# Four heads side by side in the value products of the second attention, softmax sums through GpSimd

## The chip, the cores and the metric

The kernel runs on one core of a Trainium2 chip. The metric is the device time of one execution in microseconds (us), lower is better. The median of three runs before the change is 3160.71 us (3154.86 to 3165.05).

## The reference

Eight blocks work on a residual `x` of 4 batches x 1024 tokens x 128 channels. Two of them are attentions with 16 heads. The change is in the second:

```python
def _L1_attn_a_ref(x_bld, Wq, Wkv_down, Wk_up, Wv_up, Wout):   # H, HD = 16, 64; latent 32
    q_blhd = jnp.einsum('bld,dhk->blhk', x_bld, Wq)
    latent_bll = jnp.einsum('bld,dc->blc', x_bld, Wkv_down)
    k_blhd = jnp.einsum('blc,chk->blhk', latent_bll, Wk_up)
    v_blhd = jnp.einsum('blc,chk->blhk', latent_bll, Wv_up)
    attn = jnp.einsum('bqhd,bkhd->bhqk', q_blhd, k_blhd) / jnp.sqrt(HD)
    attn = jax.nn.softmax(jnp.where(causal, attn, neg_inf), axis=-1)
    y_blhd = jnp.einsum('bhqk,bkhd->bqhd', attn, v_blhd)
    return jnp.einsum('bqhd,hdo->bqo', y_blhd, Wout)
```

## The kernel before

The blocks run one after another. Both 16-head attentions are the function `attention` with different settings (`Cfg`). In the second the up-projections are folded into the queries and the output weights, so keys and values of all heads are the same 32 latent channels (`d` = 32).

A **group** is `G` heads of one batch. `probs` holds exp(scores) transposed: a row is a key, a column a query. The keys go in 8 blocks `kb` of 128. Block `kb` has queries from `kb*128` on, so its width falls from 1024 to 128 columns, 4608 columns per head in all. The engines meet in this pattern, in which each engine's order is written out by hand:

- TensorE, per `kb`: for each head the scores (bf16; two products per half that add up pieces of the operands, and a mask product, L833, L835, L838), beside them row-maximum products for later groups (L801, into the two banks of `mx`), then `values(kb-1)` in f32 (L855). There head `j` writes the output partitions `M*j` to `M*(j+1)`, so `128/M` heads stand side by side. After block 4 `turn_max` transposes the maxima of the next group (L812).
- ScalarE: the exp of each head and block into `probs` (L910).
- VectorE: maxima of the next groups (L931 for full tiles, L935 for masked ones), then at block 4 a chain of four small steps (`finish_max`, L945 to L952) on which `turn_max` waits (`s_mc`), copies of the turned maxima (L958), and at a group's end the copy of `outp` to `osb` (L993).
- SyncE: loads up to three groups ahead, and stores.
- GpSimd does nothing inside `attention` but memsets at its start.

The sum of a row of the softmax comes from the value product itself: `vop` has the `d` value columns, one column of ones behind them (L787), and zeros up to `M`. The first attention has `G=4, M=32` with `d=8`. The second has `d=32`, which with the ones column is 33 columns, and so `G=2, M=64`. There are 16 groups of four heads in the first attention, and 32 groups of two in the second. Three batches run in a hardware loop, the fourth is unrolled behind it. In both, every group does all products of its own heads and those of the maxima of as many later heads. Before the first group lies a stretch in which only maxima are computed (24 units for the first group, 8 for the second, with `G=2`; both numbers go with `G`). A unit is one product of up to 512 columns and its maximum.

Of the kernel before, what the change touches and what calls it, by code (L numbers as in the profile page):

```python
# [606 lines left out]
class Cfg:  # L607
# [3 lines left out]
    def __init__(self, G, M, HR, SR, d, scale, k_per_head):  # L611
        self.G, self.M, self.HR, self.SR, self.d, self.scale, self.k_per_head = G, M, HR, SR, d, scale, k_per_head
        self.GN = 16 // G
        self.KG = G if k_per_head else 1
        self.rows = [(96 + 3 * HR if SR else 96), (98 + 3 * HR if SR else 98)]
        self.base = [96, 98] if SR else [0, 0]


def attention(nc, k, tag, cf, qp, kp, qs, ks, vsrc, o_scr, l_scr, m_scr):
# [9 lines left out]
    MU = 12 * G + 2  # L629

# [3 lines left out]
    NARROW_U, WIDE_U = 4 * G, 8 * G  # L634
    NPC = 8 * 4
    with ExitStack() as st:  # L636
# [5 lines left out]
        probs = c.sb("probs", [P, 2, G, T])  # L642
# [5 lines left out]
        osb = c.sb("osb", [P, 2, T])  # L648
        masked = c.sb("masked", [P, 2, CH], BF16)
# [14 lines left out]
        s_dpassed = c.sem("vector_passed")  # L664
        block = st.enter_context(nc.Block())
# [31 lines left out]
        def ahead(b, g, m):  # L697

            if isinstance(b, int) and b == NB - 1 and g + m >= GN:
                return None  # L700
            for _ in range(m):
                b, g = nxt(b, g)
            return b, g

# [13 lines left out]
        def _(sp):  # L718
# [31 lines left out]
            def store(b, g):  # L750

                wait(s_oev, b * GN + g + 2)
                for j in range(G):
# [23 lines left out]
            for i in range(2):  # L777

                sp.wait_ge(s_os[i], 16 * (G + 1) * (NB * GN // 2 + 1))

        @block.gpsimd
        def _(pool):
            pool.memset(K1[SHIFT_ROW:SHIFT_ROW + 2, :, :, :], 1.0).then_inc(s_set, 1)
            pool.wait_ge(s_set, 1)
            pool.memset(vop[:], 0.0).then_inc(s_set, 1)
            pool.wait_ge(s_set, 2)
            pool.memset(vop[:, :, :, :, d:d + 1], 1.0).then_inc(s_set, 1)  # L787

        @block.tensor
        def _(pe):  # L790
            def max_units(b, g, qts, j, u):
# [3 lines left out]
                for qt in qts:  # L795
                    for part in range(2 if qt >= 4 else 1):
# [3 lines left out]
                        pe.wait_ge(s_mxf, n * MU + u + 1)  # L800
# [5 lines left out]
            def turn_max(b, g, u):  # L806
                n = b * GN + g

                pe.wait_ge(s_mc, 4 * n + 4)
                for p in range(2):  # L810
                    pe.wait_ge(s_mxf, n * MU + u + 1)
                    pe.transpose(mx[0:G * QT, u % 2, 0:P // 2].bitcast(BF16), mpc[:, p, :], k.identb[:]).then_inc(s_mx, 1)  # L812
                    u += 1
# [27 lines left out]
            def values(b, g, kb):  # L841
# [8 lines left out]
                for half in range(2):  # L850
# [3 lines left out]
                    for j in range(G):  # L854
                        last = pe.matmul(outp[M * j:M * (j + 1), half, lo - half * CH:CH],  # L855
                                         vop[:, g % 2, kb, j % VG, :], probs[:, kb % 2, j, lo:hi],
# [3 lines left out]
            def all_max_units(b, g, parts, u):  # L860
                for qts in parts.values():
                    for j in range(G):
                        u = max_units(b, g, qts, j, u)
                return u

            await_rows0(0, 0)
            all_max_units(0, 0, WIDE, all_max_units(0, 0, NARROW, 0))
            turn_max(0, 0, NARROW_U + WIDE_U)
            await_rows0(0, 1)
            all_max_units(0, 1, NARROW, 0)  # L870

            def step(b, g):
# [6 lines left out]
                u1, u2 = NARROW_U, 0  # L879
# [13 lines left out]
                values(b, g, QT - 1)  # L893

# [3 lines left out]
        def _(act):  # L898
            act.sem_inc(s_exp, 2)

            def step(b, g):
                n = b * GN + g
                for kb in range(QT):

                    act.wait_ge(s_pv, n * 8 + kb - 1 + NPC)
                    for j in range(G):
                        u = kb * G + j
                        act.wait_ge(s_st, n * U + u + 1)
                        src = score[:, u % 2, :, :].rearrange("p h t -> p (h t)")[:, kb * P:T]
                        act.activation(probs[:, kb % 2, j, kb * P:T], src, ACT.Exp,  # L910
# [5 lines left out]
        def _(dve):  # L916
            dve.sem_inc(s_mxf, 2)
            dve.sem_inc(s_oev, 1)
            dve.sem_inc(s_os[0], 16 * (G + 1))
            dve.sem_inc(s_os[1], 16 * (G + 1))  # L920

            def reduce_units(b, g, parts, u):
                n = b * GN + g
                for qts in parts.values():
                    for j in range(G):
                        for qt in qts:
                            for part in range(2 if qt >= 4 else 1):
                                w = min((qt + 1) * P, (part + 1) * CH) - part * CH
                                dve.wait_ge(s_mx, n * MU + u + 1)
# [11 lines left out]
            def finish_max(b, g, u):  # L941
                n = b * GN + g

                dve.wait_ge(s_mxf, n * MU + u + 2)
# [9 lines left out]
            def copy_turned(b, g, u):  # L954
                n = b * GN + g
                for p in range(2):
                    dve.wait_ge(s_mx, n * MU + u + 1)
# [6 lines left out]
            def wide_maxima(b, g):  # L964
                u = reduce_units(b, g, WIDE, NARROW_U)
                finish_max(b, g, u)
                copy_turned(b, g, u)
# [8 lines left out]
            reduce_units(0, 0, NARROW, 0)  # L976
            wide_maxima(0, 0)
            reduce_units(0, 1, NARROW, 0)

            def step(b, g):  # L980
# [11 lines left out]
                dve.wait_ge(s_os[g % 2], 16 * (G + 1) * (b * (GN // 2) + g // 2 + 1))  # L992
                dve.tensor_copy(osb[:, g % 2, :], outp[:].rearrange("p h t -> p (h t)")).then_inc(s_oev, 1)  # L993

# [351 lines left out]
def layer1_attention(nc, k, ins, scr, xs):  # L1346
# [3 lines left out]
    with ExitStack() as outer:  # L1350
# [54 lines left out]
        cf = Cfg(G=2, M=64, HR=0, SR=0, d=LD, scale=0.125, k_per_head=False)  # L1405
# [1506 lines left out]
```

## Time and profile before

| | |
|---|---|
| median of 3 runs | 3160.71 us |
| the profiled execution | 3168.43 us, its span 3166.7 us |
| granted TensorE clock, mean over the span | 0.865 |
| busy: PE, DVE, ACT, POOL | 75%, 55%, 39%, 15% |
| second attention | about 1449 to 2269 us of the span |

PE is TensorE, DVE VectorE, ACT ScalarE, POOL GpSimd. The profile names a tile by its letters only, so both attentions show as `at_...`; they are told apart by the time and by the shapes (`128*32` in the value products of the first, `128*64` of the second).

### The profile page before, as it was taken

Reading aid. Unit: us, or ns where it says so; the run is one execution under the profiler, and the core shown is the slowest. Engines: PE = TensorE matmul, PEld = TensorE weight load, DVE = VectorE, ACT = ScalarE, POOL = GpSimd, SP = SyncE. Lnnn points to the kernel's source line nnn. Section 1 sums busy time; section 2 is a strip of 40 time slices with the busy share of each in tenths; the row PEclk is TensorE's granted clock in tenths of the full one; section 3 lists DMA queues with packets and bytes.
Section 4 is the critical chain, followed back from the end, with each engine's and each line's share of the span. In section 5 each row is a group of like instructions: output and inputs, shape, how many; then the busy total and the mean of one; then the engine's idle time right before and its main releaser. Section 6 shows DMA issues by size and latency. Waiting matters only on the chain. (4 is left out here: it accounts for less than half of the span.)

```text
span 3166.7 us, 46665 instructions
## 1 busy us (share of the span) xinstructions
PE 2361.7 (75%) x13512; PEld 1225.4 (39%) x13512; DVE 1743.7 (55%) x5508; ACT 1241.0 (39%) x1983; POOL 488.8 (15%) x524
## 2 busy tenths in 40 slices
PE   4559999999956328866999999999677292877382
PEld 1114344343334126532443434444254271554262
DVE  4656666666344886265665655666365324576223
ACT  2405455555534644553444444444222141343141
POOL 1400000000003000032000000000043463033554
PEclk9759999999977659877999999999888596988686
DMA  4272444443030000233122121121120152000144
GB/s 130 76 144 45 86 76 85 86 85 60 11 103 3 1 8 28 64 110 109 44 57 54 45 55 42 48 64 37 60 83 21 52 142 81 3 4 15 40 138 129
DMA packets 177903, 199.81 MB, mean 63 GB/s; under 512 B 36384, under 2 KB 117920, under 8 KB 177568
## 3 DMA queue, kind: packets, MB, share of 16 engines
q1 hardware_dynamic: 160000, 173.72, 22.1%
q0 software_dynamic: 9216, 19.02, 1.8%
q10 hardware_dynamic: 8448, 4.20, 0.4%
q8 instruction: 111, 1.82, 0.2%
q14 instruction: 128, 1.05, 0.1%
HBM read 127.09 MB, written 69.76 MB: 62 GB/s over the span
## 5 line engine op out<-in xcount | busy, mean ns | idle before, releaser
L910 ACT ACTIVATE at_probs<-at_score 128x1024 f32<-128x1024 f32 (+7 forms) x1024 | 655.2, 652 | 872.8 <-PE at_score L835 539.1
L935 DVE CUSTOM_DVE_ANT_0 at_masked<-at_mx,g_maskw 128x512 bf16<-128x512 f32 (+3 forms) x1024 | 483.4, 486 | 180.9 <-PE at_mx L801 177.6
L801 PE MATMUL at_mx<-at_K,at_Q 96*128 96x512 bf16 (+7 forms) x1536 | 467.0, 344 | 119.0 <-DVE at_mpart L935 40.9
L833 PE MATMUL at_score<-at_Q,at_K 96*128 96x512 bf16 (+7 forms) x1536 | 504.1, 332 | 28.9 <-issue 14.3
L835 PE MATMUL at_score<-at_Q,at_K 98*128 98x512 bf16 (+7 forms) x1536 | 507.2, 331 | 0.0
L931 DVE TENSOR_REDUCE at_mpart<-at_mx 128x1 f32<-128x512 f32 x512 | 353.8, 691 | 265.3 <-PE at_mx L801 245.1
L855 PE MATMUL at_outp<-at_probs,at_vop 128*32 128x512 f32 (+6 forms) x3072 | 445.2, 497 | 0.0
L801 PEld LDWEIGHTS at_mx<-at_K,at_Q 120*128 120x128 bf16 (+1 forms) x1536 | 148.4, 98 | 440.3 <-DVE at_mpart L935 198.6
L833 PEld LDWEIGHTS at_score<-at_Q,at_K 120*128 120x128 bf16 (+1 forms) x1536 | 149.8, 98 | 339.3 <-issue 183.1
L1025 POOL MEMSET n_spread<- 16x128 f32 (+1 forms) x2 | 0.7, 356 | 1541.0 <-POOLq L636 1541.0
L838 PE MATMUL at_score<-g_maskkq,g_identb 128*128 128x128 bf16 x1024 | 225.3, 220 | 0.0
L855 PEld LDWEIGHTS at_outp<-at_probs,at_vop 128*32 128x32 f32 (+1 forms) x3072 | 125.1, 122 | 108.1 <-issue 61.2
L835 PEld LDWEIGHTS at_score<-at_Q,at_K 122*128 122x128 bf16 (+1 forms) x1536 | 151.2, 98 | 22.2 <-issue 2.8
L1309 POOL TENSOR_TENSOR p_pieces<-p_rest,p_pieces 128x512 bf16<-128x512 f32 (+1 forms) x72 | 85.3, 1209 | 469.0 <-ACT p_pieces L1254 469.0
L838 PEld LDWEIGHTS at_score<-g_maskkq,g_identb 128*128 128x128 bf16 x1024 | 101.7, 99 | 52.1 <-issue 3.3
L993 DVE COPY at_osb<-at_outp 128x1024 f32<-128x1024 f32 x48 | 58.8, 1225 | 76.9 <-PE at_outp L855 76.9
L935 DVE DVE_READ_ACCUMULATOR2_ANT at_mpart<- 128x1 f32 x1024 | 85.6, 84 | 0.0
L2597 POOL DMA_INDIRECT back<-m1e_ye,m1e_target x80 | 76.8, 961 | 55.4 <-DVE m1e_ye L2588 32.6
L2597 POOL DMA_INDIRECT back<-m0e_ye,m0e_target x80 | 76.8, 960 | 55.1 <-DVE m0e_ye L2588 31.9
L1628 PE MATMUL wkv_out<-wkv_wo,wkv_y 128*128 128x128 f32 x64 | 15.0, 429 | 90.8 <-DVE b_zt L1607 54.2
L1928 POOL DMA_INDIRECT buf<-m1x_z,m1x_slot x64 | 66.7, 1042 | 78.7 <-DVE m1x_slot L2067 60.4
L1928 POOL DMA_INDIRECT buf<-m0x_z,m0x_slot x64 | 66.4, 1038 | 77.5 <-DVE m0x_slot L2067 59.3
(467 smaller groups left out, 3408.6 us busy)
## 6 DMA issues: line engine op xcount, KB each, us to landing
at_Q<-q SPq DMA_DIRECT2D x192, 128.0 KB, 3.0
at_Q<-qr SPq DMA_DIRECT2D x72, 256.0 KB, 5.9
at_K<-kr SPq DMA_DIRECT2D x72, 256.0 KB, 6.9
q<-p_pieces SPq DMA_DIRECT2D x40, 384.0 KB, 3.3
at_K<-k SPq DMA_DIRECT2D x168, 64.0 KB, 2.1
buf<-g_zeros SPq DMA_DIRECT2D x32, 325.0 KB, 5.0
o<-at_osb SPq DMA_DIRECT2D x64, 128.0 KB
n_oc<-o SPq DMA_DIRECT2D x8, 1024.0 KB, 5.0
```

The lines of the kernel that those rows point to most:

```text
L801: pe.matmul(bank[:, 0:hi - lo], Q0[0:R, g % 4, j, qt * P:(qt + 1) * P], K0[0:R, g % 4, j % KG, lo:hi], start=True, stop=True).then_inc(s_m ...
L833: pe.matmul(bank, K0[0:R0, g % 4, j % KG, kb * P:(kb + 1) * P], Q0[0:R0, g % 4, j, lo:hi], start=True, stop=False)
L835: last = pe.matmul(bank, K1[0:R1, g % 2, j % KG, kb * P:(kb + 1) * P], Q1[0:R1, g % 2, j, lo:hi], start=False, stop=not diag)
L838: last = pe.matmul(bank[:, 0:P], k.identb[:], k.maskkq[:], start=False, stop=True)
L855: last = pe.matmul(outp[M * j:M * (j + 1), half, lo - half * CH:CH], vop[:, g % 2, kb, j % VG, :], probs[:, kb % 2, j, lo:hi], start=(kb = ...
L910: act.activation(probs[:, kb % 2, j, kb * P:T], src, ACT.Exp, scale=cf.scale).then_inc(s_exp, 1)
L931: dve.reduce_max(mpart[:, part, j, qt:qt + 1], mx[:, u % 2, 0:w], AX).then_inc(s_mxf, 1)
L935: dve.tensor_tensor_reduce(masked[:, u % 2, 0:w], mx[:, u % 2, 0:w], k.maskw[:, CH - w:CH], 1.0, NEG, ALU.add, ALU.max, mpart[:, part, j, ...
L993: dve.tensor_copy(osb[:, g % 2, :], outp[:].rearrange("p h t -> p (h t)")).then_inc(s_oev, 1)
L1309: pool.tensor_tensor(pcs[n][:, g, LO, :], rest[0:it.rows, n, :], pcs[n][:, g, MID, :], ALU.subtract).then_inc(s_lo, 1)
L1928: pool.indirect_dma_start(buf, bass.IndirectOffsetOnAxis(ap=slot[:, n, t:t + 1], axis=0), z[:, t, :], None).then_inc(s_out, 16)
L2597: pool.indirect_dma_start(back, bass.IndirectOffsetOnAxis(ap=target[:, e, t:t + 1], axis=0), ye[:, e % YR, t, :], None).then_inc(s_o[e % Y ...
```

## The change

The second attention gets `G=4, M=32`. With `d` = `M` = 32 there is no room for the ones column. Instead GpSimd adds up the probabilities of key blocks 0 to 6 in a new tile `acc` (f32), four heads apart, with 4 x 6 additions a group and one that copies the first 128 columns by adding zeros. At the group's end TensorE multiplies `acc` by a block of ones (two halves of 512 columns), adds block 7 straight from `probs` (128 columns), all into the two `mx` banks, and VectorE copies both banks to `lsb`, from which SyncE stores the sums. `probs` gets a third buffer, since GpSimd reads it later than TensorE. The first attention keeps its own path. The core of the diff:

```diff
+        self.pool_sums = d == M
-    MU = 12 * G + 2
+    SU = 2 if SUMS else 0
+    MU = 12 * G + SU + 2
+    NBP = 3 if SUMS else 2
+    ADDED = 6
+        def add_probs(b, g):
+            pool = nc.gpsimd
+            n = b * GN + g
+            for kb in range(1, ADDED + 1):
+                for j in range(G):
+                    pool.wait_ge(s_exp, n * U + kb * G + j + 3)
+                    if kb == 1 and j == 0:
+                        pool.wait_ge(s_mx, earlier_sums(b, g))
+                        pool.tensor_tensor(acc[:, :, 0:P], probs[:, 0, :, 0:P],
+                                           k.zeros[:, 0:G * P].rearrange("p (j t) -> p j t", t=P), ALU.add).then_inc(s_acc, 1)
+                    if kb > 1:
+                        pool.wait_ge(s_acc, added(n, kb - 1, j))
+                    so_far = probs[:, 0, j, P:T] if kb == 1 else acc[:, j, kb * P:T]
+                    pool.tensor_tensor(acc[:, j, kb * P:T], so_far, probs[:, kb % NBP, j, kb * P:T],
+                                       ALU.add).then_inc(s_acc, 1)
...
+            def sums(b, g):
+                u = sum_at(b, g)
+                pe.wait_ge(s_acc, added(b * GN + g, ADDED, G - 1))
+                for half in range(2):
+                    pe.wait_ge(s_mxf, u + half + 1)
+                    for j in range(G):
+                        out = mx[M * j:M * (j + 1), half, :]
+                        last = pe.matmul(out, ones[:], acc[:, j, half * CH:(half + 1) * CH], start=True, stop=(half == 0))
+                    if half == 1:
+                        for j in range(G):
+                            last = pe.matmul(mx[M * j:M * (j + 1), half, CH - P:CH], ones[:],
+                                             probs[:, (QT - 1) % NBP, j, T - P:T], start=False, stop=True)
+                    last.then_inc(s_mx, 1)
...
                 values(b, g, QT - 1)
+                if SUMS:
+                    sums(b, g)
...
-                    act.wait_ge(s_pv, n * 8 + kb - 1 + NPC)
+                    act.wait_ge(s_pv, n * 8 + (kb - 1 if kb < 2 or not SUMS else max(kb - 2, 0)) + NPC)
+                    if SUMS and kb == 1:
+                        act.wait_ge(s_mx, earlier_sums(b, g))
                     for j in range(G):
+                        if SUMS and kb == 0:
+                            act.wait_ge(s_acc, added(n - 1, ADDED, j))
+                        if SUMS and kb >= 3:
+                            act.wait_ge(s_acc, added(n, max(kb - 3, 1), j))
...
                 dve.tensor_copy(osb[:, g % 2, :], outp[:].rearrange("p h t -> p (h t)")).then_inc(s_oev, 1)
+                for half in range(2 if SUMS else 0):
+                    dve.wait_ge(s_mx, sum_at(b, g) + half + 1)
+                    dve.tensor_copy(lsb[:, g % 2, half * CH:(half + 1) * CH], mx[:, half, :]).then_inc(s_mxf, 1)
...
-        cf = Cfg(G=2, M=64, HR=0, SR=0, d=LD, scale=0.125, k_per_head=False)
+        cf = Cfg(G=4, M=32, HR=0, SR=0, d=LD, scale=0.125, k_per_head=False)
```

GpSimd, inside the second attention, before: the memsets of the key rows, of `vop` and of its ones column.

```order
L783 MEMSET at_K 2x2048
L785 MEMSET at_vop 128x1024
L787 MEMSET at_vop 128x16
L636 UNCONDITIONAL_BRANCH
```

After, the start of a group's additions there (a lone number is a count, register work stands between):

```order
L826 ISA
L827 TENSOR_TENSOR at_acc<-at_probs,g_zeros 128x4x128
L832 TENSOR_TENSOR at_acc<-at_probs 128x896
...
L830 ISA
L832 TENSOR_TENSOR at_acc<-at_acc,at_probs 128x768
L823 REGISTER_ALU
L830 REGISTER_ALU
L832 TENSOR_TENSOR at_acc<-at_acc,at_probs 128x768
```

So four additions of each width from 896 down to 256 come into a queue that was empty.

TensorE, after, at the end of a group in the second attention: the last value products (L915), the sums, and the next group's first scores (L893). Before, the value products were followed by the scores at once.

```order
L915 MATMUL at_outp<-at_probs,at_vop 32x256 x4
L905 REGISTER_ALU
L915 MATMUL at_outp<-at_probs,at_vop 32x128 x4
L924 ISA
L927 REGISTER_ALU
L930 MATMUL at_mx<-at_acc,at_ones 32x512 x4
L927 REGISTER_ALU
L930 MATMUL at_mx<-at_acc,at_ones 32x512 x4
L933 MATMUL at_mx<-at_probs,at_ones 32x128 x4
L885 ISA
L893 MATMUL at_score<-at_Q,at_K 128x512
```

What moved is the start of the next group, behind three sets of products and a wait for GpSimd.

VectorE, after, at the same place; before, the two rows `at_lsb` were not there.

```order
L1085 COPY at_osb<-at_outp 128x1024
L1087 REGISTER_ALU
L1088 COPY at_lsb<-at_mx 128x512
L1087 REGISTER_ALU
L1088 COPY at_lsb<-at_mx 128x512
L1063 ISA
L1064 TENSOR_SCALAR at_vop<-a_lt 128x256
```

The copies stand ahead of all maxima of the next groups.

## Rows read from the trace of the kernel before

**Rows 1.** Windows: us, then busy us (x count) of PE, PEld, DVE, ACT, POOL, clock, DMA, GB/s

```profile
230.00:550.00 320.00, 302.89 (x2127) 129.87 (x2125) 213.19 (x679) 162.30 (x250) 0.00 (x0) 0.99 0.39 75
1480.00:1880.00 400.00, 383.23 (x2209) 159.85 (x2208) 240.70 (x772) 165.78 (x257) 0.00 (x0) 0.99 0.18 48
```

**Rows 2.** Timeline of ScalarE, second attention: start, us, instruction [idle before, releaser]

```profile
1482.34 1.02 ACT L910 ACTIVATE at_probs<-at_score 128x1024 f32<-128x1024 f32 x1 [31.66 <-PE at_score L835]
...
1507.92 1.02 ACT L910 ACTIVATE at_probs<-at_score 128x1024 f32<-128x1024 f32 x1 [1.62 <-PE at_score L835]
...
1532.36 1.02 ACT L910 ACTIVATE at_probs<-at_score 128x1024 f32<-128x1024 f32 x1 [1.61 <-PE at_score L835]
...
2249.86 1.94 ACT L910 ACTIVATE at_probs<-at_score 128x1024 f32<-128x1024 f32 x2 [1.62 <-PE at_score L835]
```

**Rows 3.** Timeline of ScalarE, first attention

```profile
225.83 1.02 ACT L910 ACTIVATE at_probs<-at_score 128x1024 f32<-128x1024 f32 x1 [78.29 <-PE at_score L835]
...
475.05 1.03 ACT L910 ACTIVATE at_probs<-at_score 128x1024 f32<-128x1024 f32 x1 [1.65 <-PE at_score L835]
...
480.91 0.92 ACT L910 ACTIVATE at_probs<-at_score 128x896 f32<-128x896 f32 x1 [0.43 <-PE at_score L835]
...
510.41 0.39 ACT L910 ACTIVATE at_probs<-at_score 128x256 f32<-128x256 f32 x1 [0.77 <-PE at_score L838]
...
515.66 1.03 ACT L910 ACTIVATE at_probs<-at_score 128x1024 f32<-128x1024 f32 x1 [2.01 <-PE at_score L835]
...
840.73 1.94 ACT L910 ACTIVATE at_probs<-at_score 128x1024 f32<-128x1024 f32 x2 [1.61 <-PE at_score L835]
...
845.12 1.79 ACT L910 ACTIVATE at_probs<-at_score 128x896 f32<-128x896 f32 x2 [0.21 <-PE at_score L835]
```

**Rows 4.** Timeline: value products of one block, second attention, then first

```profile
2263.81 1.08 PE L855 MATMUL at_outp<-at_probs,at_vop 128*64 128x512 f32 x4
...
505.89 1.07 PE L855 MATMUL at_outp<-at_probs,at_vop 128*32 128x512 f32 x8
...
511.17 0.85 PE L855 MATMUL at_outp<-at_probs,at_vop 128*32 128x384 f32 x8
```

**Rows 5.** GpSimd's additions and VectorE's beside them, by line: ns min/median/max

```profile
L1309 POOL TENSOR_TENSOR p_pieces<-p_rest,p_pieces x72: 1142/1156/1605, 49.9 to 1445.0; 128x512 bf16<-128x512 f32 x48, 32x512 bf16<-32x512 f32 x24
...
L1293 DVE TENSOR_TENSOR p_rest<-p_bank,p_pieces x48: 682/692/693, 45.5 to 1441.5; 128x512 f32<-128x512 f32 x48
...
L1293 DVE TENSOR_TENSOR p_rest<-p_lat,p_pieces x8: 1452/1478/1485, 1376.1 to 1442.5; 32x512 f32<-32x512 f32 x8
```

**Rows 6.** Timeline of a stretch with both engines at work

```profile
1397.22 2.71 POOL L1309 TENSOR_TENSOR p_pieces<-p_rest,p_pieces 128x512 bf16<-128x512 f32 x2
...
1398.12 0.72 DVE L460 SCALAR_TENSOR_TENSOR p_shift<-p_mv,p_rstd 128x4 f32<-128x4 f32 x1
1398.76 1.25 DVE L465 TENSOR_SCALAR p_ring<-g_xs,p_mv,p_rstd 128x128 f32<-128x128 f32 x1
```

**Rows 7.** Timeline of VectorE at block 4 of a group, first attention

```profile
499.05 0.18 DVE L945 TENSOR_TENSOR at_mpart<-at_mpart 128x16 f32<-128x16 f32 x1
...
499.69 0.19 DVE L952 TENSOR_TENSOR at_mpc<-at_mneg,at_mpc 128x32 bf16<-128x32 f32 x1
502.21 0.57 DVE L958 COPY at_mrow<-at_mx 32x128 bf16<-32x128 bf16 x2 [2.33 <-PE at_mx L812]
```

**Rows 8.** Timeline of the second attention up to its first group

```profile
1457.38 1.03 PE L801 MATMUL at_mx<-at_K,at_Q 96*128 96x512 bf16 x2 [18.83 <-DMA at_Q<-q]
...
1473.73 0.17 DVE L945 TENSOR_TENSOR at_mpart<-at_mpart 128x8 f32<-128x8 f32 x1
...
1480.32 0.60 PE L833 MATMUL at_score<-at_Q,at_K 96*128 96x512 bf16 x1 [0.22 <-issue]
```

**Rows 9.** Timeline: the last copy of the first attention, and of the second

```profile
870.86 1.22 DVE L993 COPY at_osb<-at_outp 128x1024 f32<-128x1024 f32 x1 [29.97 <-PE at_outp L855]
...
2267.72 1.23 DVE L993 COPY at_osb<-at_outp 128x1024 f32<-128x1024 f32 x1 [17.71 <-PE at_outp L855]
```

More of the change, by code:

```diff
@@ L641, in attention @@
         K1 = c.sb("K1", [P, 2, KG, T], BF16)
-        probs = c.sb("probs", [P, 2, G, T])
+        probs = c.sb("probs", [P, NBP, G, T])
         vop = c.sb("vop", [P, 2, QT, VG, M])
@@ L648, in attention @@
         osb = c.sb("osb", [P, 2, T])
+        if SUMS:
+            acc = c.sb("acc", [P, G, T])
+            ones = c.sb("ones", [P, 32])
+            lsb = c.sb("lsb", [P, 2, T])
         masked = c.sb("masked", [P, 2, CH], BF16)
@@ L703, in ahead, with sum_at, earlier_sums, added @@
             return b, g
+        def sum_at(b, g):
+            n = b * GN + g
+            if ahead(b, g, 2):
+                return (n + 2) * MU + SUM_U
+            return NB * GN * MU + (2 if g == GN - 1 else 0)
+        def earlier_sums(b, g):
+            n = b * GN + g
+            if ahead(b, g, 1):
+                return (n + 1) * MU + SUM_U + 2
+            return NB * GN * MU + 2
+        def added(n, kb, j):
+            return (n + 1) * AU + 1 + (kb - 1) * G + j + 1
         def over_batches(eng, step):
@@ L752, in store @@
                 wait(s_oev, b * GN + g + 2)
+                if SUMS:
+                    sp.dma_start(o_scr[ds(g * G * d, G * d), ds(first_token(b), T)], osb[:, g % 2, :]).then_inc(s_os[g % 2], 16)
+                    wait(s_mxf, sum_at(b, g) + 4)
+                    sp.dma_start(l_scr[ds(g * G, G), ds(first_token(b), T)],
+                                 lsb[0:(G - 1) * M + 1:M, g % 2, :]).then_inc(s_os[g % 2], 16)
+                    return
                 for j in range(G):
@@ L783, in _ @@
             pool.memset(K1[SHIFT_ROW:SHIFT_ROW + 2, :, :, :], 1.0).then_inc(s_set, 1)
+            if SUMS:
+                pool.wait_ge(s_set, 1)
+                pool.memset(ones[:], 1.0).then_inc(s_set, 2)
+                pool.sem_inc(s_acc, AU)
+                over_batches(pool, add_probs)
+                return
             pool.wait_ge(s_set, 1)
@@ L804, in max_units, with turn_max @@
                 return u
-            def turn_max(b, g, u):
+            def turn_max(b, g, u, off=0):
                 n = b * GN + g
@@ L855, in values, with all_max_units @@
                         last = pe.matmul(outp[M * j:M * (j + 1), half, lo - half * CH:CH],
-                                         vop[:, g % 2, kb, j % VG, :], probs[:, kb % 2, j, lo:hi],
+                                         vop[:, g % 2, kb, j % VG, :], probs[:, kb % NBP, j, lo:hi],
                                          start=(kb == 0), stop=(kb == (3 if half == 0 else 7)))
                 last.then_inc(s_pv, 1)
-            def all_max_units(b, g, parts, u):
+            def sums(b, g):
[11 more added lines that the diff above has]
+                    last.then_inc(s_mx, 1)
+            def all_max_units(b, g, parts, u, off):
                 for qts in parts.values():
                     for j in range(G):
-                        u = max_units(b, g, qts, j, u)
+                        u = max_units(b, g, qts, j, u, off)
                 return u
+            if SUMS:
+                pe.sem_inc(s_mx, 2 * SU)
+                pe.wait_ge(s_set, 3)
             await_rows0(0, 0)
-            all_max_units(0, 0, WIDE, all_max_units(0, 0, NARROW, 0))
-            turn_max(0, 0, NARROW_U + WIDE_U)
+            all_max_units(0, 0, NARROW, 0, 2 * SU)
+            all_max_units(0, 0, WIDE, WIDE_AT, SU)
+            turn_max(0, 0, WIDE_AT + WIDE_U, SU)
             await_rows0(0, 1)
-            all_max_units(0, 1, NARROW, 0)
+            all_max_units(0, 1, NARROW, 0, SU)
             def step(b, g):
@@ L962, in copy_turned, with wide_maxima @@
                     u += 1
[L964 to L967, printed above, removed]
+            def wide_maxima(b, g, off=0):
+                u = reduce_units(b, g, WIDE, WIDE_AT, off)
+                finish_max(b, g, u, off)
+                copy_turned(b, g, u, off)
             def values(b, g):
```

45 lines of the change are left out of this document (26 added, 19 removed).

## The prediction

> **What bounds the kernel now.** I read the windows first. In both attentions TensorE is the busy engine: 303 of 320 us in the first and 383 of 400 us in the second, at a granted clock of 0.99, while VectorE is at 67% and 60%, ScalarE at 51% and 41%, and GpSimd has no work at all [rows 1]. So a gain has to come out of TensorE's own products, and GpSimd is free for what is added.
>
> Next I looked for the price of the same work at the new setting, and the trace holds it: the first attention runs with four heads side by side. Its groups of four heads start every 40.61 us (475.05 to 515.66) [rows 3]. In the second, groups of two heads start every 24.44 us (1507.92 to 1532.36), so four heads cost 48.9 us [rows 2]. The reason is in the value products. Four records of two heads take 1.08 us for a block of 512 columns, and eight records of four heads take 1.07 us [rows 4]. Standing side by side is nearly free, so four heads in one go halve this part. The rest of a group (scores, masks, maxima, exps) has the same shapes in both, and the number of contraction rows (96 or 120) leaves no trace in the starts above that I would have to correct for.
>
> **The change part by part.** All is counted from the second attention's first exp to the end of its last copy from `outp`. Before, that is 2267.72 + 1.23 - 1482.34 = 786.6 us [rows 2, 9].
>
> *Groups at the new width.* I take the first attention as it stands: 15 groups from the first exp to the first exp of the last group, 840.73 - 225.83 = 614.9 us, loop ends included [rows 3]. The same stretch of the second was 2249.86 - 1482.34 = 767.5 us [rows 2].
>
> *Sums on TensorE.* Each group gets 512 + 512 + 128 columns of four heads side by side, f32, behind value products of the same shape. Going from 384 to 512 columns adds 0.22 us [rows 4], so 1152 columns are 9 x 0.22 = 2.0 us. 15 groups: +30 us.
>
> *Copies of the sums on VectorE.* Two copies of 512 columns. A copy of 1024 takes 1.23 us [rows 9], so each is about 0.65 us. They run while TensorE does the next group's first scores, and only then are the `mx` banks wanted again. Cost: nothing. Without that cover it would be 1.3 us a group.
>
> *Additions on GpSimd.* The nearest row is a two-input operation of 512 columns, 1142 ns at least and 1156 in the median, with one input and the output in bf16 [rows 5]. I take 1.15 us for 512 columns, all of it per column: 2.25 ns. A group has 4 x (896 + 768 + 640 + 512 + 384 + 256) = 13,824 columns, 31.05 us, and 1.15 us for the copy of 512: 32.2 us in one queue, against about 42 us a group. Bounds: if part of the 1.15 us is fixed, wide ones are cheaper (30 us). Nothing here shows all-f32 operands, so above I allow 30% more.
> Does it end in time? I count from the group's first exp. The first add waits for the exp of block 1, head 0, which ends at 480.91 + 0.92 - 475.05 = 6.8 [rows 3]. From there the queue is full, since exps come earlier than their additions (block 6 is complete at 510.41 + 0.39 - 475.05 = 35.8 [rows 3], its turn is at 36.7). Block 2 is done at 22.9, block 3 at 28.7, block 6 at 39.0. TensorE wants the sums where the next group would start, about 1.2 us before its first exp (my estimate): 40.6 - 1.2 = 39.4. So it is just in time, with 0.4 us to spare.
>
> *The waits of VectorE beside GpSimd.* This is where most is taken back. Beside GpSimd's operations of 1.1 us, a VectorE operation on 512 columns with two inputs from SBUF took 1478 ns, while one that reads `p_bank` from PSUM took 692, never more than 693 [rows 5]. At 1398.12 an operation on 4 columns took 0.72 us, and the one behind it, on 128 columns with one tensor input, 1.25 us, which is as long as the GpSimd operation that had started between them [rows 6]. So such a step waits until the running GpSimd operation is over, and the next one again. The chain of four steps from L945 to L952 is of this kind: all operands in SBUF, 0.2 us each when GpSimd is idle [rows 7]. It starts at 499.05 - 475.05 = 24.0, in the middle of block 3, whose additions of 640 columns take 1.44 us. The first step waits to 24.4, and each of the other three waits out one whole addition: the chain ends at 29.4 instead of 24.8. TensorE reaches `turn_max` only 2.33 us after the chain's end today [rows 7], which is cover, and 4.6 - 2.3 = 2.3 us of TensorE stand still. Behind the waiting transposition stand `values(3)` and all of blocks 5 to 7. 15 groups: +34.5 us. Bounds: 0 (steps on so few columns slip through) and 4 us a group (all four wait, the cover has gone).
> The same wait is weighed against the Trainium skill. Its page "SBUF — State Buffer", section "Who interferes with whom", says that VectorE operations with two SBUF inputs, and copies, casts and tensor_scalar in a two-port mode, share a port pair with GpSimd, that it is held for a whole instruction, and that the other blocks. That names all four steps of the chain, and by it the term stays as it stands. The rows show it for three kinds, not for a cast. By rows alone, with the cast free, the term would be 0.85 us a group, 13 us.
>
> *The groups at the end.* The last group has no maxima beside it, so TensorE is through early (870.86 - 840.73 = 30.1 us after the first exp [rows 3, 9]), but GpSimd needs 845.12 + 0.93 - 840.73 = 5.3, then 32.2 us: the sums start at 37.5, take 2.0, and the last copy 0.65: 40.2 us. Before it was 19.1 us (two heads). The last but one has no narrow maxima and waits some 1.3 us for GpSimd.
>
> *The stretch before the first group.* 24 units take 1473.73 - 1457.38 = 16.35 us, 0.68 each, paced by VectorE [rows 8]. 32 units become 64: +21.8 us. Nothing hides it. Other things there (larger but fewer loads, fewer memsets) are within 2 us and not counted.
>
> *Not on the path.* The third `probs` buffer relaxes a wait of ScalarE on value products, but ScalarE's starts are released by the scores [rows 2, 3], so it brings nothing. Fewer and larger stores leave SyncE's queue. Its new wait for the sums stands ahead of the loads for two groups later, which have 40 us.
>
> *Sum.* 614.9 + 30 + 34.5 + 1.3 + 40.2 = 720.9, less 786.6: -65.7. Plus 21.8: **-44 us**. The profiled execution would go from 3168.4 to 3124. The median of the runs lies 8 us below it, and 3160.7 - 44 gives **3117 us**.
>
> **The rivals.**
> 1. *The small steps slip through.* Then the 34.5 us go, and GpSimd still ends at 39.0 against 39.4. The last but one group waits 3.3 us. -76 us, **3084**. For it: they read few columns and might be served between two additions. Against it: 0.72 us on 4 columns [rows 6].
> 2. *The additions set the pace (the other side).* With the stall above, TensorE wants the sums at 41.7, GpSimd has them at 39.0 plus 0.6 for the gaps in which the chain runs. That is 6% of room. Above it each further per cent costs 0.32 us in every group, 5 us in all. At 2.6 ns a column (15% dearer than the row) the whole gain is gone, at 30% it is 75 us worse than that, **3235**. For it: f32 in and out where the row has bf16, and two semaphore waits ahead of most additions. Against it: the row's 32-partition and 128-partition forms cost the same, and its spread is small.
> 3. *The masked maxima wait too.* L935 reads PSUM and the mask from SBUF. If it took part in the contention, some 24 of 32 a group would lose about 0.7 us each, 17 us, of which VectorE's idle third could hide little because two banks tie it to TensorE: 3250 to 3350, say **3310**. Against it: the 692 ns of the PSUM form beside GpSimd, 693 at most [rows 5].
> 4. *The heads do not overlap.* If the products of four heads ran as slowly as two by two, the values stay as they were and only costs remain: **3240**. Against it stands the first attention itself [rows 4].
>
> **How the numbers follow.** Forecast (chain waits, additions just fit): 0.56, by itself 3100 to 3135. Rival 1: 0.22, 3075 to 3100. Additions a little dearer, gain mostly eaten, 3135 to 3160: 0.08. Rival 2 beyond the balance: 0.09. Rival 3: 0.04. Rival 4: 0.01. The range 3076 to 3155 leaves out the slower cases and little of the others. A measurement here tells about 0.3% (9.5 us) from no change. Slower takes rivals 2 to 4, 0.13 with a part near the balance, same gets 0.04, faster 0.83.
>
> **What would show it.** In the profile after: groups of the second attention start every 44.9 us (42.6 by rival 1, over 46 by rival 2); GpSimd about 32 us busy a group, 512-column additions near 1.15 us; the four steps of the chain, 1 us and more each instead of 0.18, and TensorE idle at `turn_max` with VectorE as releaser (forecast) or idle before the sums with GpSimd as releaser (rival 2); masked maxima as long as before (not rival 3); the four-head value products at 1.07 us a block of 512; the last group waiting some 7 us for GpSimd; the first exp 22 us later. I am wrong if additions in f32 cost over 2.4 ns a column or if the chain falls in a gap of GpSimd's.

## The result: slower by 2.3%, and the profile after

The changed kernel takes **3233.3 us** (median of 4 runs, 3221.1 to 3247.5) against 3160.9 us: ratio 1.0231, 95% interval 1.0208 to 1.0254. The forecast was 3117 us. The profiled execution took 3223.8 us, the first row of its page:

```profile
span 3222.0 us, 47805 instructions
PE 2302.9 (71%) x13864; PEld 1198.9 (37%) x13864; DVE 1858.6 (58%) x5412; ACT 1239.3 (38%) x1983; POOL 1032.6 (32%) x923
```

In the timeline of ScalarE in the second attention, the first exp of four groups (start, us, instruction):

```profile
1499.09 1.02 ACT L1002 ACTIVATE at_probs<-at_score 128x1024 f32<-128x1024 f32 x1 [52.42 <-PE at_score L895]
...
1607.14 1.02 ACT L1002 ACTIVATE at_probs<-at_score 128x1024 f32<-128x1024 f32 x1 [3.59 <-PE at_score L895]
...
1660.42 1.02 ACT L1002 ACTIVATE at_probs<-at_score 128x1024 f32<-128x1024 f32 x1 [3.58 <-PE at_score L895]
...
2032.44 1.02 ACT L1002 ACTIVATE at_probs<-at_score 128x1024 f32<-128x1024 f32 x1 [3.56 <-PE at_score L895]
...
2080.09 1.02 ACT L1002 ACTIVATE at_probs<-at_score 128x1024 f32<-128x1024 f32 x1 [3.57 <-PE at_score L895]
```

Groups of four heads were to start every 44.9 us. Some do so every 47.65 (2032.44 to 2080.09), most every 52 to 58 (1607.14 to 1660.42: 53.28). Over the 15 intervals, 1499.09 to 2284.11, that is 785.0 us where 680.7 were forecast.

Where the time goes in such a group shows in its timeline on all engines:

```profile
1623.39 17.98 POOL L832 TENSOR_TENSOR at_acc<-at_acc,at_probs 128x768 f32<-128x768 f32 x12
...
1631.03 10.37 DVE L1037 TENSOR_TENSOR at_mpart<-at_mpart 128x16 f32<-128x16 f32 x1
...
1641.43 0.18 DVE L1040 TENSOR_SCALAR at_mneg<-at_mpart 128x32 f32<-128x32 f32 x1
1641.65 0.18 DVE L1042 CAST at_mpc<-at_mneg 128x32 bf16<-128x32 f32 x1
1641.87 0.19 DVE L1044 TENSOR_TENSOR at_mpc<-at_mneg,at_mpc 128x32 bf16<-128x32 f32 x1
...
1642.19 0.39 PE L872 MATMUL at_mx<-g_identb,at_mpc 128*32 128x128 bf16 x2 [8.20 <-DVE at_mpc L1044]
...
1642.31 2.41 PE L915 MATMUL at_outp<-at_probs,at_vop 128*32 128x128 f32 x16
```

The four steps of the chain (L945 to L952 in the kernel before) are L1037 to L1044 here. The first one, on 16 columns, took 10.37 us, and the other three 0.2 each. GpSimd ran twelve additions without a gap from 1623.39 to 1641.37, and the step ended at 1641.40. So VectorE didn't wait for the addition that was running. It waited for the whole row of additions, the running one and seven more, until GpSimd had no work left. GpSimd ran dry because TensorE stood still behind the chain (8.20 us at `turn_max`) and made no more scores for ScalarE; its next addition came 5.18 us later, and ScalarE had released it:

```profile
1646.55 6.06 POOL L832 TENSOR_TENSOR at_acc<-at_acc,at_probs 128x384 f32<-128x384 f32 x7 [5.18 <-ACT at_probs L1002]
```

Another group's timeline shows the forecast's own picture, each step waiting out one addition:

```profile
1849.34 1.02 DVE L1037 TENSOR_TENSOR at_mpart<-at_mpart 128x16 f32<-128x16 f32 x1
...
1850.39 1.47 DVE L1040 TENSOR_SCALAR at_mneg<-at_mpart 128x32 f32<-128x32 f32 x1
...
1851.90 1.46 DVE L1042 CAST at_mpc<-at_mneg 128x32 bf16<-128x32 f32 x1
...
1853.39 1.46 DVE L1044 TENSOR_TENSOR at_mpc<-at_mneg,at_mpc 128x32 bf16<-128x32 f32 x1
...
1854.98 0.40 PE L872 MATMUL at_mx<-g_identb,at_mpc 128*32 128x128 bf16 x2 [2.69 <-DVE at_mpc L1044]
```

That is 4 of the 15 groups; 11 are of the first kind, I will say locked out. By line and shape, 1500 to 2330 us (busy us, mean ns | idle before), and the wait at `turn_max` (us, times, longest):

```profile
L832 POOL TENSOR_TENSOR at_acc<-at_probs 128x896 f32<-128x896 f32 x64 | 131.4, 2084 | 0.0
L1037 DVE TENSOR_TENSOR at_mpart<-at_mpart 128x16 f32<-128x16 f32 x15 | 118.0, 7868 | 0.5
...
L832 POOL TENSOR_TENSOR at_acc<-at_acc,at_probs 128x512 f32<-128x512 f32 x64 | 78.8, 1259 | 0.0
...
L832 POOL TENSOR_TENSOR at_acc<-at_acc,at_probs 128x256 f32<-128x256 f32 x64 | 45.5, 722 | 11.3 <-ACT at_probs L1002 10.2 <-POOL at_acc L832 0.4
```

```profile
PE at_mx L872 <- DVE at_mpc L1044: 100.3, 15, 8.2
```

The windows answer to [rows 1] (busy us (x count) of PE, PEld, DVE, ACT, POOL, then the clock):

```profile
1560.00:1960.00 400.00, 329.08 (x2226) 138.43 (x2224) 286.03 (x669) 158.50 (x242) 260.42 (x188) 0.89 0.18 47
1631.00:1642.00 11.00, 2.80 (x20) 0.89 (x12) 10.86 (x4) 2.18 (x4) 10.36 (x8) 0.72 0.00 0
1642.00:1660.00 18.00, 16.88 (x131) 7.43 (x131) 10.47 (x38) 4.60 (x12) 6.69 (x8) 0.79 0.02 6
1607.00:1631.00 24.00, 23.60 (x156) 9.98 (x154) 17.58 (x49) 13.81 (x16) 17.01 (x10) 1.00 0.36 90
2062.00:2080.00 18.00, 17.06 (x132) 7.35 (x133) 10.69 (x38) 4.61 (x12) 11.30 (x12) 0.81 0.04 13
```

TensorE is down from 383 to 329 busy us in 400, and its granted clock from 0.99 to 0.89. Before the stall a group runs at 1.00, and for the rest of it at 0.79, so partly at 1.2 GHz instead of 2.4. This holds behind the short stall too (last row, 0.81). The stall is paid twice: the sixteen value products right behind it took 2.41 us (1642.31). Without the additions (first experiment below) the same sixteen take 1.35 us, 1616.98 to 1618.33.

The last group answers to [rows 9]. Its sums waited for GpSimd and then ran slower (the same 16 products took 1.89 us at 1551.11):

```profile
2323.58 3.64 PE L930 MATMUL at_mx<-at_acc,at_ones 128*32 128x512 f32 x16 [5.56 <-POOL at_acc L832]
...
2327.72 0.69 DVE L1088 COPY at_lsb<-at_mx 128x512 f32<-128x512 f32 x1 [1.44 <-PE at_mx L933]
```

### The profile page after: what moved, and what is told of

It reads as the page before. It is cut to its first block and busy times, and to the rows that moved or that the text cites. A ratio compares the mean times of both kernels' runs of the same rounds, so it can differ in the third digit from the quotient of the medians.

```text
span 3222.0 us, 47805 instructions
## 1 busy us (share of the span) xinstructions
PE 2302.9 (71%) x13864; PEld 1198.9 (37%) x13864; DVE 1858.6 (58%) x5412; ACT 1239.3 (38%) x1983; POOL 1032.6 (32%) x923
## 5 line engine op out<-in xcount | busy, mean ns | idle before, releaser
L861 PE MATMUL at_mx<-at_K,at_Q 96*128 96x512 bf16 (+7 forms) x1536 | 486.0, 354 | 124.9 <-DVE at_mpart L1027 42.1
L893 PE MATMUL at_score<-at_Q,at_K 96*128 96x512 bf16 (+7 forms) x1536 | 513.9, 338 | 32.1 <-ACT at_probs L1002 13.6
L895 PE MATMUL at_score<-at_Q,at_K 98*128 98x512 bf16 (+7 forms) x1536 | 517.0, 337 | 0.0
L832 POOL TENSOR_TENSOR at_acc<-at_acc,at_probs 128x768 f32<-128x768 f32 (+4 forms) x320 | 395.0, 1264 | 66.8 <-ACT at_probs L1002 65.4
L915 PE MATMUL at_outp<-at_probs,at_vop 128*32 128x512 f32 (+3 forms) x3072 | 318.4, 525 | 1.0 <-ACT at_probs L1002 1.0
L893 PEld LDWEIGHTS at_score<-at_Q,at_K 120*128 120x128 bf16 (+1 forms) x1536 | 152.0, 99 | 293.4 <-issue 155.2
L832 POOL TENSOR_TENSOR at_acc<-at_probs 128x896 f32<-128x896 f32 x64 | 131.4, 2084 | 0.0
L1037 DVE TENSOR_TENSOR at_mpart<-at_mpart 128x16 f32<-128x16 f32 x32 | 121.0, 3781 | 1.1
L915 PEld LDWEIGHTS at_outp<-at_probs,at_vop 128*32 128x32 f32 x3072 | 80.6, 113 | 74.5 <-issue 47.7
L827 POOL TENSOR_TENSOR at_acc<-at_probs,g_zeros 128x512 f32<-128x512 f32 x16 | 20.3, 1269 | 265.8 <-ACT at_probs L1002 265.8
L1085 DVE COPY at_osb<-at_outp 128x1024 f32<-128x1024 f32 x32 | 39.2, 1225 | 95.5 <-PE at_outp L915 95.5
```

Of the source, the lines that this page charges most:

```text
L832: pool.tensor_tensor(acc[:, j, kb * P:T], so_far, probs[:, kb % NBP, j, kb * P:T], ALU.add).then_inc(s_acc, 1)
L861: pe.matmul(bank[:, 0:hi - lo], Q0[0:R, g % 4, j, qt * P:(qt + 1) * P], K0[0:R, g % 4, j % KG, lo:hi], start=True, stop=True).then_inc(s_m ...
L893: pe.matmul(bank, K0[0:R0, g % 4, j % KG, kb * P:(kb + 1) * P], Q0[0:R0, g % 4, j, lo:hi], start=True, stop=False)
L895: last = pe.matmul(bank, K1[0:R1, g % 2, j % KG, kb * P:(kb + 1) * P], Q1[0:R1, g % 2, j, lo:hi], start=False, stop=not diag)
L1037: dve.tensor_tensor(mpart[:, 0, :, 4:8], mpart[:, 0, :, 4:8], mpart[:, 1, :, 4:8], ALU.max).then_inc(s_mc, 1)
```

## The experiments

Times are medians. The kernel before, run on the same chip each time, took 3160 to 3163 us.

**No additions.** `acc` is filled with ones once, and GpSimd adds nothing, so the stored sums are not those of the softmax:

```diff
-                over_batches(pool, add_probs)
+                pool.memset(acc[:], 1.0).then_inc(s_acc, 1)
+                pool.wait_ge(s_acc, AU + 1)
+                pool.sem_inc(s_acc, AU * NB * GN + AU)
```

> The changed kernel without GpSimd's additions: acc is filled once with ones, so the stored softmax sums are not those of the reference; TensorE's products for the sums, the copies and all else stay. Theory (GpSimd's additions keep VectorE's four-step chain out, and the clock falls behind the stall): the chain's steps take 0.18 us again, groups start every 42.6 us as in the first attention plus 2.0 us, clock 0.99 in the attention, about 3082 us in all, 78 below the kernel before. Rival (four heads side by side or the sums on TensorE cost what the change lost): stays above 3160 us.

3077.9 us, ratio 0.9731 (0.9710 to 0.9751). Timelines of ScalarE (two group starts) and of VectorE (the chain's first step), and a window from that step on:

```profile
1548.11 1.02 ACT L1004 ACTIVATE at_probs<-at_score 128x1024 f32<-128x1024 f32 x1 [3.59 <-PE at_score L897]
...
1590.19 1.02 ACT L1004 ACTIVATE at_probs<-at_score 128x1024 f32<-128x1024 f32 x1 [3.59 <-PE at_score L897]
```

```profile
1571.99 0.17 DVE L1039 TENSOR_TENSOR at_mpart<-at_mpart 128x16 f32<-128x16 f32 x1
```

```profile
1571.00:1589.00 18.00, 16.79 (x156) 7.30 (x154) 11.36 (x43) 7.01 (x17) 0.00 (x0) 1.00 0.01 4
```

Groups start every 42.1 us where the forecast has 42.6 without the chain's wait, and each step of the chain takes 0.2. So the price of four heads side by side held. The additions cost the changed kernel 155 us, though TensorE's products waited for their results only once, in the last group. What the forecast says of GpSimd being just in time isn't tested here.

**Each addition waits for the one before**, the smallest edit that opens gaps in GpSimd's row:

```diff
-                    if kb > 1:
-                        pool.wait_ge(s_acc, added(n, kb - 1, j))
+                    pool.wait_ge(s_acc, added(n, kb, j) - 1)
```

> The changed kernel, but each GpSimd addition first waits for the one before it. Theory that VectorE is kept out because the next addition is taken up before the last has let go: with a gap behind each addition every chain step waits for one addition at most, the first step under 1.6 us in all 15 groups (after the change 10.4 us in 11 of them), groups every 48 to 49 us, about 3175 us. Rival (GpSimd simply wins when both ask): the 10.4 us waits stay, and the time is 3233 us or more.

3201.8 us, 1.0127 (1.0109 to 1.0145): 31 us less than the changed kernel, by an edit that only adds waits. Its timeline of VectorE in a group, and two groups by line:

```profile
1621.02 0.46 DVE L1036 TENSOR_TENSOR at_mpart<-at_mpart 128x16 f32<-128x16 f32 x1
1621.51 0.18 DVE L1039 TENSOR_SCALAR at_mneg<-at_mpart 128x32 f32<-128x32 f32 x1
1621.73 1.40 DVE L1041 CAST at_mpc<-at_mneg 128x32 bf16<-128x32 f32 x1
1623.16 0.19 DVE L1043 TENSOR_TENSOR at_mpc<-at_mneg,at_mpc 128x32 bf16<-128x32 f32 x1
```

```profile
L831 POOL TENSOR_TENSOR at_acc<-at_acc,at_probs 128x512 f32<-128x512 f32 x64 | 81.1, 1267 | 6.1
...
L929 PE MATMUL at_mx<-at_acc,at_ones 128*32 128x512 f32 x256 | 57.8, 1054 | 74.9 <-POOL at_acc L831 74.9
```

No step took over 1.53 us in any of the 15 groups. With 0.1 us between additions (6.1 us in 64), two or three steps pass from one gap on before a step waits again. So the lock-out did not come beside a row with gaps. But the additions, now later, are waited for in all 16 groups (74.9 us), so this version doesn't reach the forecast.

**GpSimd pauses for the chain**: block 3's additions wait until the chain is done.

```diff
+                if kb == 3 and ahead(b, g, 1):
+                    pool.wait_ge(s_mc, 4 * n + 8)
```

> The changed kernel with one more wait: GpSimd starts the additions of key block 3 only after VectorE's chain for the next group's maxima is done. All the additions remain. Theory: the chain's steps take 0.18 us in all 15 groups, no wait at turn_max; GpSimd's 34.8 us plus about 1.2 us then end some 3 us after TensorE wants the sums, groups every 46 us, about 3152 us. Rival (the additions themselves set the pace from the start): groups stay at 48 to 53 us and the time at 3200 us or more, since GpSimd only gets later.

3163.4 us, 1.0003 (0.9991 to 1.0015). Taking all waits out of the chain, the lock-outs and the waits for one addition alike, gave 70 us, net of what the pause costs elsewhere. The four steps take 0.2 us each, and groups about 47.5. By line, GpSimd waited 23.3 us in all, and TensorE now waits for GpSimd's results:

```profile
L834 POOL TENSOR_TENSOR at_acc<-at_acc,at_probs 128x640 f32<-128x640 f32 x64 | 96.7, 1538 | 23.3 <-DVE at_mpc L1046 23.3
...
L932 PE MATMUL at_mx<-at_acc,at_ones 128*32 128x512 f32 x256 | 51.8, 951 | 52.9 <-POOL at_acc L834 52.9
```

That is rival 2's mechanism, which stood hidden behind the lock-out. I expected 3152; the slower sums behind their wait (951 ns a product instead of 633, with a clock of 0.94 over 1520 to 1960 us) were not in it.

**The same, and GpSimd adds blocks 1 to 4 only**; TensorE sums up blocks 5 to 7 itself.

```diff
-    ADDED = 6
+    ADDED = 4
...
-                            last = pe.matmul(mx[M * j:M * (j + 1), half, CH - P:CH], ones[:],
-                                             probs[:, (QT - 1) % NBP, j, T - P:T], start=False, stop=True)
+                        for kb in range(ADDED + 1, QT):
+                            for j in range(G):
+                                last = pe.matmul(mx[M * j:M * (j + 1), half, kb * P - CH:CH], ones[:],
+                                                 probs[:, kb % NBP, j, kb * P:T], start=False, stop=(kb == QT - 1))
```

> As the kernel with the wait, and GpSimd adds up only key blocks 0 to 4; blocks 5, 6 and 7 go straight from probs into the sums on TensorE (640 columns more of four heads, about 1.1 us a group). ScalarE waits for the earlier sums one block earlier. Theory: GpSimd is done at 36 us of a group, before it is wanted at 39.4; groups every 43.7 us, about 3102 us, under the kernel before by 58 us. Rival (additions at any time slow VectorE or TensorE): 3150 us or more.

**3107.3 us, 0.9819 (0.9797 to 0.9840)**: 1.8% faster than the kernel before. Groups take about 44.3 us, and the window 1520 to 1960 us has a clock of 0.96.

**Four blocks without the pause.**

> The changed kernel with the additions of blocks 5 and 6 left out on GpSimd; TensorE takes these blocks' sums straight from the probabilities, as it does for block 7 (some 640 columns more, about 1.1 us a group). Nothing in it keeps GpSimd from adding beside VectorE's chain. Theory (VectorE is kept out until GpSimd's row of additions ends, which with or without blocks 5 and 6 is after block 4): the first step of the chain stays at about 10 us in most groups, groups stay at 48 to 56 us, and only the last group gets shorter: 3205 to 3240 us, forecast 3225. Rival (GpSimd simply had too much to do, and with a quarter less it is in time): groups under 45.5 us, 3100 to 3130, as with the wait for the chain added.

3237.4 us, 1.0246 (1.0219 to 1.0273), no better than the changed kernel. Ten of 15 groups are locked out, for the same 10.4 us, by line:

```profile
L1038 DVE TENSOR_TENSOR at_mpart<-at_mpart 128x16 f32<-128x16 f32 x15 | 108.7, 7246 | 0.5
```

So too much work for GpSimd was not the cause. With a fifth less (6.9 of 34.9 us a group) the loss stays; only after the lock-out is gone does the lighter load pay (56 us between the two versions with the pause).

**Four blocks, each addition waiting for the one before.**

> The version above, and each addition waits for the one before it. GpSimd's work a group is 4 x (2.08 + 1.81 + 1.54 + 1.26) + 1.3 + 16 gaps of 0.1 = 29.7 us, well below 44. Theory (what locks VectorE out is that an addition is taken up before the one ahead is over, and each step costs at most one addition when they are apart): the four steps together 2 to 3 us, inside the cover of 2.3, groups 44.3 to 45.5 us, 3105 to 3125 us, forecast 3110. Rival (additions beside the chain cost more than their duration, in TensorE or ScalarE too): above 3140.

3114.4 us, 0.9853 (0.9825 to 0.9881). Two ways to break the row, a pause and gaps, end within 7 us of one another.

**Additions alone, in the kernel before.** If the row of additions is the cause, it must hurt where nothing else is changed. In every group of two heads GpSimd runs seven additions that nothing reads, over the chain in one version (they wait for the exps of block 2, as shown) and behind it in another (block 5 instead):

```diff
+                    pool.wait_ge(s_exp, n * U + 2 * G + G + 2)
+                    for i in range(BURST):
+                        pool.tensor_tensor(junk[:, i, :], k.zeros[:, 0:640], k.zeros[:, 0:640], ALU.add).then_inc(s_junk, 1)
```

> The kernel before with nothing changed but GpSimd: in every group of two heads seven additions of 640 columns each, one behind another without a wait between them, on arrays of their own that nothing reads. They start once the exps of block 2 are there and last 7 x 1.53 = 10.7 us, so they lie over the chain of four steps on VectorE. Theory (VectorE is locked out until a row of additions ends): one of the four steps takes 4 to 8 us where it took 0.2 us, TensorE stands still for some 2 to 6 us of that in each of 31 groups, 60 to 190 us in all: 3220 to 3350, forecast 3290. If each step waits out just one addition: 4 x 1.4 - 2.3 of cover = about 3 us, with no step above 1.6 us: 3230 to 3260. If the long step of the changed kernel came from something else in that kernel (its extra semaphore traffic, its sums): steps of 0.2 us, no change.

> The same seven additions, started once the exps of block 5 are there, so behind the chain of this group and over before that of the next. Theory (only what waits for the chain pays): four steps of 0.2 us as before, 3155 to 3180. Rival (additions on GpSimd slow the rest of the kernel by their traffic in SBUF as such): as much slower as the version with the burst over the chain, above 3220.

Over the chain 3269.5 us, 1.0334 (1.0292 to 1.0375); behind it 3169.1 us, 1.0019 (1.0006 to 1.0031). So work beside the chain costs 107 us and the same work behind it 7. But the timeline of VectorE over the burst shows no lock-out; each step waits out one addition (1.25 us here), in all 31 groups with a burst over the chain:

```profile
1521.82 0.60 DVE L960 TENSOR_TENSOR at_mpart<-at_mpart 128x8 f32<-128x8 f32 x1
1522.46 1.18 DVE L963 TENSOR_SCALAR at_mneg<-at_mpart 128x16 f32<-128x16 f32 x1
1523.68 1.18 DVE L965 CAST at_mpc<-at_mneg 128x16 bf16<-128x16 f32 x1
1524.89 1.18 DVE L967 TENSOR_TENSOR at_mpc<-at_mneg,at_mpc 128x16 bf16<-128x16 f32 x1
```

My theory had this wrong: a row without gaps is not enough for the lock-out, though no run has it beside a row with gaps.

**What else the lock-out needs** was tried in two ways. First, the burst over the chain with two different operands, and then also in place and with two waits, already met, ahead of each addition:

> The burst over the chain again, in the kernel before, but each addition reads two different arrays, as those of the changed kernel do, so that one should take 1.53 us where 1.25 was measured with the same array read twice. Seven of them lie from about 0.7 us before block 2's turn on, 10.7 us, with some 6.5 us left when the chain starts. If the long step of the changed kernel hangs on two different operands or on the longer duration: a first step of 6 to 7 us in most groups, 3280 to 3330 us. If not: four steps of 0.6 to 1.5 us that each wait out one addition, the whole 5 us, about 1.2 us a group more than with the short additions: 3290 to 3310 us, with no step above 1.6 us.

> The same, and each addition is in place (it adds to the array it writes) and has two semaphore waits ahead of it that are already met, one on ScalarE's counter and one on an earlier addition, as in the changed kernel. If the lock-out comes with such waits or with the in-place form: a first step of 6 to 7 us, followed by three of 0.2, in most groups. If it comes from none of these: four steps that each wait out one addition, as in the version above, and what decides between the two kinds stays open.

3333.4 us, 1.0548 (1.0523 to 1.0572), and 3341.7 us, 1.0574 (1.0548 to 1.0600). The additions take 1.53 us, the first step 0.2 to 0.35 and the others 1.46 each; no lock-out in 31 groups of each. Second, the place in an addition at which the first step comes:

```diff
+                if kb == 2:
+                    pool.tensor_tensor(junk[:], k.zeros[:, 0:448], k.zeros[:, 0:448], ALU.add)
```

> The changed kernel with one more GpSimd addition a group, of 448 columns to an array that nothing reads, ahead of the additions of block 2 (some 0.9 us). Nothing else changes; GpSimd has more to do. In the changed kernel the first of the four steps came with 0.9 to 1.0 us of the running addition to go and was locked out in 11 of 15 groups; in the kernels with a burst it came with 0.2 to 0.6 us to go and never was. Here it comes with about 0.4 us to go. Theory (where in an addition the first step comes decides whether it gets in at its end): no step over 1.6 us in nearly all groups, groups of 47.5 to 48.5 us, 3155 to 3180 us, forecast 3165, although GpSimd does more. Rival (the lock-out hangs on the changed kernel's additions themselves): first steps of about 10 us as before, 3233 to 3250 us.

3238.2 us, 1.0244 (1.0227 to 1.0261): 12 of 15 groups locked out. The timeline of VectorE in two groups:

```profile
1524.88 11.25 DVE L1040 TENSOR_TENSOR at_mpart<-at_mpart 128x16 f32<-128x16 f32 x1
...
1578.96 0.42 DVE L1040 TENSOR_TENSOR at_mpart<-at_mpart 128x16 f32<-128x16 f32 x1
```

> The kernel before with the burst of additions on two different arrays over the chain, and one addition of 384 columns ahead of them (some 0.75 us), so that the first of the four steps comes with about 0.95 us of the running addition to go instead of 0.25. Theory of the place in the addition: a first step of 6 to 8 us, followed by three of 0.2 us, in at least a third of the groups; 3335 to 3420 us. Rival (place does not matter; a row without gaps of seven additions alone never locks out): first step about 1 us, next three 1.46, as before; 3335 to 3365 us.

3362.3 us, 1.0634 (1.0607 to 1.0661): first step 1.0 us, the next three 1.46, none of 31 locked out. The place doesn't decide. But the row moved by 0.9 us, and the locked step grew from 10.4 to 11.3 us: its length is that of the rest of the row.

The bursts show the clock's part as well. Windows of the burst with one operand and with two:

```profile
1520.00:2240.00 720.00, 623.17 (x3498) 257.69 (x3496) 469.35 (x1217) 262.24 (x410) 218.77 (x180) 0.97 0.16 44
```

```profile
1520.00:2240.00 720.00, 616.90 (x3245) 249.59 (x3242) 447.80 (x1128) 242.63 (x378) 251.61 (x168) 0.90 0.14 41
```

TensorE waits 2.7 us a group for the chain in the one (70.9 us, 26 times) and 3.2 in the other (77.8, 24 times). Over 31 groups that differs by 16 us, but the times differ by 64, and the granted clock is 0.90 instead of 0.97.

## Why the prediction was wrong, step by step

- **The step that failed** is in the waits of VectorE beside GpSimd: "The first step waits to 24.4, and each of the other three waits out one whole addition". In 4 groups exactly this happened: chain of 5.5 us (1849.34 to 1854.85), forecast 5.4, and TensorE standing still for 2.7, forecast 2.3. The close 5.4 is in part luck: the first step waited 1.0 us instead of 0.4, and the other three took 1.46 each where the forecast leaves about 1.6. In 11 groups the first step waited out the whole row instead, and TensorE stood still for 8.2 us. The stretch of [rows 6], from which I took the rule, does have rows without gaps, of five operations, and there each step waited out one. GpSimd's timeline in the kernel before:

```profile
1393.87 6.06 POOL L1309 TENSOR_TENSOR p_pieces<-p_rest,p_pieces 128x512 bf16<-128x512 f32 x5 [4.04 <-ACT p_pieces L1254]
```

So the rule was right for those rows and for the bursts, and nothing in them announced the lock-out. The bounds, 0 and 4 us a group, came from the same rows and were too narrow for the same reason. By the Trainium skill ("SBUF — State Buffer", "Who interferes with whom") the port pair is held for a whole instruction. The trace agrees in the 4 groups. The page does not say who gets the pair next when another GpSimd instruction is already queued. In the 11 the trace shows it: VectorE was kept out over eight instructions in a row.

Its size: the 11 locked intervals have a mean of 54.4 us, the three other whole ones 47.6. Part of these 6.7 us is not the lock-out's: the ends of two batches fell into locked intervals, and they are longer without additions too (45.0 and 46.8 us). Against the same places of the version without additions (43.3 and 42.5) it is 11.1 and 5.2, so a lock-out costs 5.95 us more than four waits for one addition: 11 x 5.95 = 65 us.

- **The clock was left out.** Groups that waited out one addition a step took 47.6 us, forecast 44.9, and 5.2 us more than at the same places without additions. Of these 2.7 are the wait. The other 2.5 go with a clock of 0.81 in the 18 us behind it, where it is 1.00 without additions; no run changes the clock alone. The forecast has 2.3 us a group and 1.3 once. Over 15 intervals that is 42 us too little. With the 65, and 3 us that the groups without additions were cheaper than forecast, it makes the 104 us that the 15 intervals are over.
- **The additions were mis-sized**: 1259 ns for 512 columns and 34.9 us a group (4 x (2.084 + 1.809 + 1.535 + 1.259 + 0.994 + 0.722) + 1.27), forecast 1.15 and 32.2. From 896 to 256 columns the time falls by 1362 ns, 2.13 ns a column, and some 0.18 us are fixed. In the changed kernel this cost little, since stalled groups leave GpSimd time; with the chain let through TensorE waited 52.9 us for the sums (the version with the pause). The forecast named over 2.4 ns a column as a sign of being wrong. It was 2.43 (33.6 us for 13,824 columns), yet that is not what failed in the changed kernel.
- **Right**: the stretch before the first group. From the first product of the maxima (1452.60) to the first exp (1499.09) it is 46.5 us against 25.0 [rows 8], so +21.5, forecast +21.8. But that product came 4.8 us earlier than before, and so the first exp only 16.8 us later where 22 were forecast; the reason is open. Groups without additions take 42.1 us, forecast 42.6, with 2.3 us of sums on TensorE, forecast 2.0. No instruction waited for the copies of the sums. The masked maxima are unchanged (686 ns, rival 3 out). In the version without additions a value product of 512 columns takes 596 ns, as in the first attention (rival 4 out). The last group took 44.3 us instead of 40.2: it waited 5.6 for GpSimd (forecast some 7), at dearer additions and a lower clock.
- **The rivals.** None had the lock-out. Rival 2 gave nearly the right time (3235) for a wrong reason: in the changed kernel TensorE's products waited for sums once. Taking 13% for slower was too little for a step whose rule came from shorter rows of other operations.

**Shown:** the additions cost 155 us. Most of that comes from VectorE's four small steps being kept out beside a row of additions without gaps; either a pause or gaps end the lock-out; less work for GpSimd alone doesn't. **Argued:** the share of the clock, which only goes along with the stalls. **Open:** what decides between lock-out and one addition a step. Duration, different operands, in-place form, waits already met, and place in the addition each failed to bring it about in the kernel before, where four or five additions of the burst were left when the chain began; in the changed kernel eight or more were. Not tried: a longer row ahead of the chain, a first step of 16 columns there instead of 8, and arrays at the changed kernel's addresses.

## What to carry to other kernels

Work given to an idle GpSimd is not free if VectorE has a short dependent chain of all-SBUF steps on TensorE's path. Unless a trace shows the chain beside such a row, allow for two prices: one instruction a step, and the whole row of GpSimd work that is queued. Let GpSimd pause there (23 us of waits for GpSimd made the kernel 70 us faster). Fix the wait and the load together: neither alone was faster than the kernel before, both together were, by 1.8% with the pause and 1.5% with gaps. To a stall of TensorE add what it loses in clock behind it.

## What the runs showed of the hardware that was not expected

- A VectorE operation on 16 columns with two inputs, 0.18 us alone, took 10.3 to 11.3 us beside an unbroken row of GpSimd additions in 33 of 45 groups of three kernels, and 0.4 to 1.0 us in the others.
- With a wait of each addition on the one before, which costs 0.1 us each, this came in 0 of 30 groups of two kernels.
- A stall of TensorE of 3.2 us a group instead of 2.7 came with a granted clock of 0.90 instead of 0.97 over 720 us.
- An addition of 640 columns takes 1.25 us with one array read twice and 1.53 with two.
